# Fills and small transfers moved out of the first stage of a six-part transformer kernel

## The chip, the cores and the metric

The kernel runs on one core of one Trainium2 chip. The time is that of the device, in microseconds: 2439.63 us for the kernel before (median of 3 runs, 2437.85 to 2439.83). The core has five engines that run side by side and meet at semaphores: TensorE (PE in the profile; its weight loads are PEld), VectorE (DVE), ScalarE (ACT), GpSimd (POOL) and SyncE (SP), which here only issues transfers (DMAs).

## What is computed

The input x has 4 batches of 512 rows of 128 numbers; a context has 4 batches of 77 rows, a condition 4 rows. Four blocks follow each other, each added to x:

```python
x = x + slots(cond, ctx, layernorm(x))      # 3 steps of slot attention over the context, with a small MLP
x = x + experts(layernorm(x))               # 8 experts of 128 -> 512 -> 128, each row goes to its best 2
x = x + layers(layernorm(x), cond, ctx, masks)   # 6 layers: self attention (16 heads of 8), cross attention, MLP
x = x + ternary_mlp(x)                      # quantised 128 -> 512 -> 128

# in the slots, before the steps:
x_in  = layernorm(ctx) * g + b;  k = x_in @ wk + bk;  v = x_in @ wv + bv
slots = q_mu + exp(q_logsig) * layernorm(x)
# in the layers:
scores = where(mask, -inf, q @ k.T / sqrt(8))
```

## The kernel before, in words

x, the running state and most tables stay in SBUF for the whole kernel, as 16 tiles of 128 rows. `build` calls six stages one after the other: `load_and_prepare`, `slot_steps`, `route_tokens`, `some_experts` (the body of a loop with two turns of four experts each, so every instruction in it runs twice), `begin_layers` and `layers` (six layers, ordered by a planner, and the last MLP at its end). Each stage has a block with one program per engine. It ends when all engines are through; then GpSimd clears the stage's semaphores and a barrier follows (`stage`, L145). Inside a stage an engine runs its list in order and stops only at `wait_ge`.

**The first stage**, `load_and_prepare`:
- SyncE (L160 to L170) issues the loads in this order: x, ctx, slot rows, slot columns, slot matrices, and six constants (cond, condT, cos, sin, mask, cmask) that count up the semaphore `consts` to 96. Then (L172 to L187) it waits for VectorE's mask products, writes them to scratch in HBM, waits for that, and copies rows into the key stacks: from `shift_rows` (three partitions of -1) and from the scratch mask, 20 small transfers in all.
- GpSimd makes the identity, fills `shift_rows` (L200), small tables, the context key stack kc6 (L211), the query stacks q6 and cq (L216, four fills of 32 partitions each with ones), and the value buffers vaug and vcaug (L217 to L220). `q6`, `cq`, `vaug` and `vcaug` are first used in the layers.
- VectorE (from L262): small fills; then `dve.wait_ge(consts, 96)` and the two mask products (L267, L268); then the statistics of the context (`row_statistics`, whose lines are those of its helpers: L90, L93 moments, L100 to L102 the seed of a reciprocal root, L108 to L110 three steps of it), its normalised rows (L124), the same for the 16 tiles of x, the first slots (L282, L283), a bias (L285), and last the slots' values (L287), for which it waits for TensorE.
- TensorE turns the context and multiplies it with the key and value matrices (L243 to L255); ScalarE copies and adds biases between (L229 to L236).

**The slot steps** have no program for SyncE. VectorE starts them with L455 on the state. Every step passes the four batches from VectorE to GpSimd (roots), TensorE, ScalarE and back; L500 adds a step's output.

**The experts** have no program for GpSimd. SyncE loads the weights of four experts into `big` (L641, L642), TensorE waits for each, multiplies up (L656), ScalarE applies the gelu (L682), TensorE multiplies down (L665) and VectorE adds the share of the output to the state (L694). VectorE starts with a copy of the four experts' shares (L686).

`shift_rows` lies in the first three partitions of `big`, which the slot steps and the experts overwrite.

Of the kernel before, what the change touches and what calls it, by code (L numbers as in the profile page):

```python
# [147 lines left out]
def load_and_prepare(nc, a, m, sem):  # L148
# [2 lines left out]
    ident, ident0, lnx, lnc, ctx_ps, ctx_sb, kv_ps, kv_sb = (sem(n) for n in (  # L151
        "identity", "identity_zero", "noise_ready", "ctx_normal", "ctx_turned", "ctx_copied", "kv_ready", "kv_copied"))
    sig, dch, pch = sem("sigma"), sem("prep_dve"), sem("prep_pool")
    vu_ps, neg, neg_out, shift_out = sem("value_ready"), sem("neg_mask"), sem("neg_mask_out"), sem("shift_rows_out")
    stack0, ones = sem("stack_zero"), sem("stack_one")

    with nc.Block() as block:
        @block.sync
        def _(sp):
            sp.dma_start(m.x[:], a["x"].rearrange("b (t p) d -> p (b t) d", p=P)).then_inc(x_in, 16)  # L160
            sp.dma_start(m.ctx[0:N_CTX], a["ctx"].rearrange("b n d -> n b d")).then_inc(ctx_in, 16)
            sp.dma_start(m.rows0[:], a["slot_rows"].partition_broadcast(P)).then_inc(rows_in, 16)
            sp.dma_start(m.cols0[:], a["slot_cols"]).then_inc(mats, 16)
            sp.dma_start(m.mats0[:], a["slot_mats"]).then_inc(mats, 16)
            sp.dma_start(m.cond_rows[:], a["cond"].rearrange("b d -> (b d)").partition_broadcast(P)).then_inc(consts, 16)
            sp.dma_start(m.condT[:], a["condT"]).then_inc(consts, 16)
            sp.dma_start(m.cs[:, 0, :], a["cos"]).then_inc(consts, 16)
            sp.dma_start(m.cs[:, 1, :], a["sin"]).then_inc(consts, 16)
            sp.dma_start(m.mask_u8[:], a["mask"]).then_inc(consts, 16)
            sp.dma_start(m.cmask_u8[:], a["cmask"]).then_inc(consts, 16)  # L170

            sp.wait_ge(neg, 2)  # L172
            sp.dma_start(a["neg_mask"], m.negmask[:]).then_inc(neg_out, 16)
            sp.dma_start(a["neg_cmask"], m.negcmask[:]).then_inc(neg_out, 16)
            sp.wait_ge(neg_out, 32)

            sp.wait_ge(stack0, 1)
            sp.wait_ge(pch, 1)
            for u in range(2):
                shift, mask = u * ROW_BLOCK + ROW_SHIFT, u * ROW_BLOCK + ROW_MASK  # L180
                for i in range(2):
                    sp.dma_start(m.k6[shift:shift + 3, i], m.shift_rows[:]).then_inc(shift_out, 16)
                for b in range(B):
                    sp.dma_start(m.kc6[shift:shift + 3, b, :, 0:N_CTX], m.shift_rows[:, :, 0:N_CTX]).then_inc(shift_out, 16)
                    sp.dma_start(m.kc6[mask:mask + 1, b, :, 0:N_CTX],
                                 a["neg_cmask"][b:b + 1, :].unsqueeze(1).to_broadcast([1, PAIRS, N_CTX])).then_inc(shift_out, 16)
            sp.wait_ge(shift_out, 2 * 16 * (2 + 2 * B))  # L187
            sp.wait_ge(consts, 96)

        @block.gpsimd  # L190
        def _(pool):
            chain = Chain(pool, pch)
            pool.memset(m.ident[:], 0.0).then_inc(ident0, 1)
            pool.wait_ge(ident0, 1)
            pool.affine_select(out=m.ident[:], in_=m.ident[:], compare_op=ALU.not_equal, fill=1.0, base=0,
                               pattern=[[-1, P]], channel_multiplier=1).then_inc(ident, 1)
            pool.wait_ge(ident, 1)
            pool.tensor_copy(m.ident_bf[:], m.ident[:]).then_inc(ident, 1)

            chain.link(pool.memset(m.shift_rows[:], -1.0))  # L200

            chain.link(pool.memset(m.tri[:], 1.0))
            chain.link(pool.affine_select(out=m.tri[:], in_=m.tri[:], compare_op=ALU.is_ge, fill=0.0, base=0,
                                          pattern=[[1, P]], channel_multiplier=-1))

            chain.link(pool.memset(m.minus_half[:], -0.5))
            for e in range(EXPERTS):
                last = pool.memset(m.prefer[:, e:e + 1], float(EXPERTS - e))
            chain.link(last)

            pool.memset(m.kc6[:].rearrange("p b i n -> p (b i n)").bitcast(F32), 0.0).then_inc(stack0, 1)  # L211
            pool.wait_ge(stack0, 1)
            for q in (m.q6[:].rearrange("p i h n -> p (i h n)"), m.cq[:].rearrange("p h n -> p (h n)")):
                flat = q.bitcast(F32)
                for u in range(2):
                    chain.link(pool.memset(flat[u * ROW_BLOCK + 32:(u + 1) * ROW_BLOCK], TWO_ONES))  # L216
            chain.link(pool.memset(m.vaug[:], 0.0))  # L217
            chain.link(pool.memset(m.vcaug[:], 0.0))
            chain.link(pool.memset(m.vaug_heads[:, :, :, :, 16 + HD:17 + HD], 1.0))
            chain.link(pool.memset(m.vcaug_heads[0:N_CTX, :, :, 16 + HD:17 + HD], 1.0))  # L220

        @block.scalar
        def _(act):
# [36 lines left out]
        def _(dve):  # L260
# [2 lines left out]
            dve.memset(m.ones32[:], 1.0)  # L263
            dve.memset(m.minus_round[:], -ROUND)
            chain.link(dve.memset(m.ones[:], 1.0))
            dve.wait_ge(consts, 96)
            dve.tensor_scalar(m.negmask[:], m.mask_u8[:], MASKED, None, ALU.mult).then_inc(neg, 1)  # L267
            dve.tensor_scalar(m.negcmask[:], m.cmask_u8[:], MASKED, None, ALU.mult).then_inc(neg, 1)  # L268
            dve.wait_ge(ctx_in, 16)
            row_statistics(dve, chain, m.ctx[0:N_CTX], B, D, m.st)  # L270
            for b in range(B):
# [10 lines left out]
            chain.link(dve.tensor_tensor(m.hat[:], m.hat[:], m.sigma[:].unsqueeze(1).to_broadcast([P, T, D]), ALU.mult))  # L282
            chain.link(dve.tensor_tensor(m.state[:], m.hat[:], m.rows0[:, 0:1, :].to_broadcast([P, T, D]), ALU.add))  # L283

            dve.tensor_tensor(m.cond_rows[:], m.cond_rows[:], m.rows0[:, 5:6, :].to_broadcast([P, B, D]), ALU.add).then_inc(lnx, 1)  # L285
            dve.wait_ge(vu_ps, 1)
            dve.tensor_tensor(m.slot_v[0:N_CTX, :, 0:D], m.ps[0:N_CTX, 4, :].rearrange("n (b d) -> n b d", b=B),  # L287
# [3 lines left out]
def slot_steps(nc, a, m, sem):  # L291
# [2 lines left out]
             "root_m", "hat_m", "turned_m", "in_m", "h_ps", "h", "out_ps", "moments_p", "root_p", "hat_p", "gained", "dve", "pool")  # L294
    (moments_q, root_q, hat_q, turned_q, in_q, q_ps, q_sb, logits, mx, probs, attn, upd, moments_m, root_m, hat_m, turned_m, in_m,
     h_ps, h_sb, out_ps, moments_p, root_p, hat_p, gained, dch, pch) = [sem(f"sl_{n}") for n in names]
    scale = float(np.float32(1.0) / np.float32(D ** -0.5))

    def count(s, b):
# [3 lines left out]
        return v[:, b * TB:(b + 1) * TB]  # L303

    with nc.Block() as block:
        @block.tensor
        def _(pe):
            def turn(s, b, hat, turned):
# [323 lines left out]
def some_experts(nc, a, m, sem, turn):  # L632

    (h_ps, h_sb, o_ps, o_sb, share) = [sem(n) for n in ("ex_h_ready", "ex_h", "ex_out_ready", "ex_added", "ex_share")]
    w_in = [sem(f"ex_weights{u}") for u in range(AT_ONCE)]
    steps = [(u, b) for u in range(AT_ONCE) for b in range(B)]
    with nc.Block() as block:
        @block.sync
        def _(sp):
# [2 lines left out]
                sp.dma_start(m.proj[:, u], a["c_proj"][turn * AT_ONCE + u]).then_inc(w_in[u], 16)  # L642
            for u in range(AT_ONCE):
                sp.wait_ge(w_in[u], 32)

        @block.tensor
        def _(pe):
# [1365 lines left out]
def build(nc, a):  # L2013
    with ExitStack() as ctx:
# [40 lines left out]
        m.cmask_u8 = sb("cmask_u8", [B, N_CTX], U8)  # L2055
        m.negmask = sb("negmask", [B, S], BF16)
        m.negcmask = sb("negcmask", [B, N_CTX], BF16)
        m.shift_rows = big[0:3, 0:PAIRS * S // 2].bitcast(BF16).rearrange("r (i n) -> r i n", i=PAIRS)
        m.tri = sb("tri", [P, P], BF16)
        m.ones = sb("ones", [P, P], BF16)  # L2060
        m.invsum = {kind: sb(f"invsum_{kind}", [P, TB * 4, 2]) for kind in ("self", "cross")}
# [41 lines left out]
        m.left = m.hat[:, 2 * TB:4 * TB, :].rearrange("p (i t) d -> p i (t d)", i=2)  # L2103
        m.unit = m.xnT[:, 2:4, :]
        m.rot = sb("rot", [P, 2, 2, S])
        m.rparts = sb("rparts", [P, 2, 3, S], BF16)
        m.rot_c = sb("rot_c", [P, 2, NC_ALL])[:]
        m.rparts_c = m.cond_rows[:].rearrange("p b d -> p (b d)").bitcast(BF16)[:, 0:3 * NC_ALL].rearrange("p (k n) -> p k n", k=3)
# [119 lines left out]
```

## Time and profile before

| | before |
|---|---|
| median of 3 runs | 2439.63 us |
| the profiled execution's own time | 2435.36 us |
| its span, first to last instruction | 2433.6 us |
| TensorE busy | 2031.6 us (83%) |
| VectorE busy | 1689.8 us (69%) |
| ScalarE busy | 1537.7 us (63%) |
| GpSimd busy | 865.7 us (36%) |
| mean granted clock of TensorE | 0.919 |

The span runs from the first to the last instruction; the device's time of the same execution has a little around it (1.8 us). Busy shares are means over stages with different limits. In the rows, "L216" is line 216 of the kernel, "q<-" says what is written and from what, "x2" how many instructions a row merges; a row that merges several gives the time from the first one's start to the last one's end.

### The profile page before, as it was taken

How to read it: one execution, taken by the hardware profiler on the slowest of the kernel's cores; microseconds unless marked ns; L12 is line 12 of the kernel's file. 1: busy time of each engine (PE TensorE's matmuls, PEld its weight loads, DVE VectorE, ACT ScalarE, POOL GpSimd, SP SyncE). 2: the span in 40 equal slices, each digit the busy share in tenths (PEclk: the TensorE clock that was granted, in tenths of full speed). 3: DMA queues.
4: the chain of work that ended last, by engine and by line, in shares of the span. 5: the costliest groups of instructions: out<-in, count | busy, mean ns of one | idle time of the engine just before them, and what ended most of it. 6: DMA issues, size and time to landing. Idle time of an engine off the chain costs nothing.

```text
span 2433.6 us, 38335 instructions
## 1 busy us (share of the span) xinstructions
PE 2031.6 (83%) x14062; PEld 894.9 (37%) x14066; DVE 1689.8 (69%) x3124; ACT 1537.7 (63%) x1937; POOL 865.7 (36%) x1354
## 2 busy tenths in 40 slices
PE   2654799926889999999999999999999999988651
PEld 1332576711223333333433333333333333333321
DVE  6776211136678888888878888788878888886456
ACT  1432233303568888788778887888788878868442
POOL 4443000012234435434444344344443444433331
PEclk9776899966899999999999999999999999999665
DMA  1000101032133344332253334432353334321100
GB/s 48 1 0 1 35 1 34 0 78 56 38 65 82 80 89 84 80 88 67 68 91 88 81 82 79 92 75 61 70 108 88 74 74 93 84 54 36 32 6 9
DMA packets 148642, 144.40 MB, mean 59 GB/s; under 512 B 30887, under 2 KB 136163, under 8 KB 148451
## 3 DMA queue, kind: packets, MB, share of 16 engines
q1 hardware_dynamic: 148463, 142.05, 26.2%
q8 instruction: 108, 1.77, 0.3%
q14 instruction: 71, 0.58, 0.1%
HBM read 79.01 MB, written 60.51 MB: 57 GB/s over the span
## 4 chain that ended last, share of the span: by engine, by line
PE 56%; DVE 14%; ACT 4%; issue 3%; POOL 1%; DMA 1%; SPq 0%; POOLq 0%; DVEq 0%; ACTq 0%
PE ps L1265 14%; PE ps L1229 7%; PE ps L1218 6%; DVE smax L1763 6%; PE ps L1343 5%; PE ps L1384 4%; PE ps L1375 4%; PE ps L1277 4%; ACT big L1498 2%; PE ps L1318 2%; DVE rot L1779 2%; PE ps L1302 2%; PE ps L1240 1%; PE ps L1252 1%; PE ps L1335 1%
## 5 line engine op out<-in xcount | busy, mean ns | idle before, releaser
L1498 ACT ACTIVATE big<-ps 128x1024 f32<-128x1024 f32 x960 | 955.5, 1026 | 262.3 <-PE ps L1229 243.1
L1763 DVE TENSOR_REDUCE smax<-ps 128x2 f32<-128x1024 f32 x768 | 921.7, 1221 | 266.7 <-PE ps L1218 261.1
L1265 PE MATMUL ps<-big,vaug 128*32 128x512 f32 x3072 | 412.4, 615 | 2.9 <-ACT big L1498 2.9
L1218 PE MATMUL ps<-k,q 49*128 49x512 bf16 x1536 | 296.8, 395 | 63.7 <-DVE smax L1763 33.7
L1229 PE MATMUL ps<-q,k 52*128 52x512 bf16 x1536 | 296.5, 388 | 11.2 <-DVE smax L1763 5.4
L1694 POOL CAST mparts<-smax 128x16 bf16<-128x16 f32 x96 | 19.4, 202 | 578.1 <-DVE smax L1763 578.1
L1218 PEld LDWEIGHTS ps<-k,q 49*128 49x128 bf16 x1536 | 73.1, 94 | 313.5 <-DVE smax L1763 105.0
L694 DVE SCALAR_TENSOR_TENSOR state<-ps,share,state 128x128 f32<-128x128 f32 x128 | 36.0, 344 | 200.3 <-PE ps L665 200.3
L682 ACT ACTIVATE big<-ps 128x512 f32<-128x512 f32 x128 | 76.5, 598 | 142.9 <-PE ps L656 142.9
L1770 DVE TENSOR_REDUCE maxima<-ps 128x8 f32<-128x616 f32 x192 | 144.6, 794 | 30.7 <-PE ps L1252 29.1
L1343 PE MATMUL ps<-xnT,w 128*128 128x512 f32 x288 | 164.9, 658 | 0.9 <-ACT xnT L1535 0.9
L1229 PEld LDWEIGHTS ps<-q,k 52*128 52x128 bf16 x1536 | 75.3, 94 | 194.5 <-issue 89.9
L656 PE MATMUL ps<-xnT,big 128*128 128x512 f32 x256 | 118.0, 606 | 24.3 <-DMA big<-in_c_proj 24.3
L665 PEld LDWEIGHTS ps<-big 128*128 128x128 f32 x1024 | 119.1, 192 | 14.3 <-issue 14.3
L1685 POOL TENSOR_TENSOR hat<-rot,rparts 128x512 f32<-128x512 f32 x72 | 83.5, 1160 | 112.8 <-ACT rparts L1546 112.8
L665 PE MATMUL ps<-big 128*128 128x128 f32 x1024 | 119.2, 275 | 0.0
L1277 PE MATMUL ps<-big,vcaug 128*32 128x512 f32 x768 | 105.7, 621 | 14.2 <-ACT big L1498 7.6
L1681 POOL TENSOR_TENSOR rot<-rot 128x512 f32<-128x512 f32 x72 | 91.3, 1269 | 70.4 <-DVE rot L1779 69.0
L1667 POOL TENSOR_SCALAR var_next<-mv_next 128x4 f32<-128x4 f32 x24 | 5.6, 233 | 306.6 <-DVE mv_next L1828 306.6
L1384 PE MATMUL ps<-w,hT 128*128 128x128 f32 x768 | 109.6, 287 | 1.6 <-ACT hT L1571 1.6
L1375 PE MATMUL ps<-xnT,w 128*128 128x512 f32 x192 | 107.5, 657 | 1.9 <-ACT xnT L1535 1.9
L1691 POOL TENSOR_TENSOR rparts<-hat,rparts 128x512 bf16<-128x512 f32 x72 | 83.3, 1157 | 69.8 <-ACT rparts L1550 69.8
(290 smaller groups left out, 3026.7 us busy)
## 6 DMA issues: line engine op xcount, KB each, us to landing
q<-scratch_queries SPq DMA_DIRECT2D x48, 384.0 KB, 6.3
k<-scratch_keys SPq DMA_DIRECT2D x48, 384.0 KB
cq<-scratch_cross_queries SPq DMA_DIRECT2D x48, 384.0 KB, 5.8
scratch_queries<-rparts SPq DMA_DIRECT2D x24, 384.0 KB, 2.4
scratch_keys<-rparts SPq DMA_DIRECT2D x24, 384.0 KB, 2.6
scratch_cross_queries<-rparts SPq DMA_DIRECT2D x24, 384.0 KB, 2.5
scratch_queries<-rparts SPq DMA_DIRECT2D x24, 256.0 KB, 2.7
scratch_keys<-rparts SPq DMA_DIRECT2D x24, 256.0 KB, 3.0
```

Of the source, the lines that this page charges most:

```text
L656: nc.tensor.matmul(m.ps[:, n % 4, :], m.fc[:, u, c * P:(c + 1) * P], m.xnT[:, b, :], start=True, stop=True).then_inc(h_ps, 1)
L665: last = nc.tensor.matmul(m.ps[:, 4 + i % 2, t * P:(t + 1) * P], m.hT[:, i % 2, c, t * P:(t + 1) * P], m.proj[:, u, c, :], start=(c == 0), ...
L1218: last = nc.tensor.matmul(out[:, u], m.q6[rows, v % 2, 2 * g + pr, qt * P:(qt + 1) * P], m.k6[rows, v % 2, 2 * g + pr, :], start=True, sto ...
L1229: last = nc.tensor.matmul(out[:, u], m.k6[rows, v % 2, 2 * g + pr, kt * P:(kt + 1) * P], m.q6[rows, v % 2, 2 * g + pr, :], start=True, sto ...
L1265: last = nc.tensor.matmul(m.ps[32 * j:32 * j + 32, pv_bank, :], of_head(m.vaug, v % 2 * TB + kt, g, j), of_quad("self", q)[:, j, :], start ...
L1277: last = nc.tensor.matmul(m.ps[32 * j:32 * j + 32, aux, :], of_head(m.vcaug, v % B, g, j), of_quad("cross", n)[:, j, :], start=(g % 2 == 0 ...
L1343: got = nc.tensor.matmul(banks(kind, i)[:, half, :], w_of(m, names[half]), m.xnT[:, xn[of_turn, i], :], start=True, stop=True)
L1375: nc.tensor.matmul(banks("up", 2 * v + c // 2)[:, c % 2], w_of(m, "f1")[:, c * P:(c + 1) * P], m.xnT[:, xn["ff", v], :], start=True, stop= ...
L1384: last = nc.tensor.matmul(m.ps[:, aux, t * P:(t + 1) * P], m.hT1[:, c, t * P:(t + 1) * P], w_of(m, "f2")[:, c * P:(c + 1) * P], start=(c = ...
L1498: nc.scalar.activation(of_quad(kind, p // 2)[:, p % 2 * 2:p % 2 * 2 + 2, :], banks("exp" if kind == "self" else "cross exp", p), ACT.Exp, ...
L1763: nc.vector.tensor_reduce(m.smax[:, n % 2, qt, :, pr], banks("max", i), AX.X, ALU.max).then_inc(s_read["self"], 1)
L1770: nc.vector.tensor_reduce(m.maxima[:, qt, :, PAIRS // 2 * half:PAIRS // 2 * (half + 1)], banks("cross max", i)[:, :, 0:PAIRS // 2 * N_CTX] ...
```

## The change

The four query-stack fills and the four fills of the value buffers go from GpSimd's program in the first stage to a new GpSimd program in the experts' stage, which is executed in both turns. The 22 small transfers go from SyncE's program in the first stage to a new one in the slot steps. The mask products go from the head of VectorE's program, with their wait for `consts`, to a place behind the first slots. `shift_rows` moves from `big` to `rot`, which is first used in the layers.

```diff
@@ load_and_prepare, sync @@
-            sp.wait_ge(neg, 2)
-            sp.dma_start(a["neg_mask"], m.negmask[:]).then_inc(neg_out, 16)
-            sp.dma_start(a["neg_cmask"], m.negcmask[:]).then_inc(neg_out, 16)
-            sp.wait_ge(neg_out, 32)
-
-            sp.wait_ge(stack0, 1)
-            sp.wait_ge(pch, 1)
-            for u in range(2):
...
-            sp.wait_ge(shift_out, 2 * 16 * (2 + 2 * B))
             sp.wait_ge(consts, 96)
@@ load_and_prepare, gpsimd @@
-            pool.memset(m.kc6[:].rearrange("p b i n -> p (b i n)").bitcast(F32), 0.0).then_inc(stack0, 1)
-            pool.wait_ge(stack0, 1)
-            for q in (m.q6[:].rearrange("p i h n -> p (i h n)"), m.cq[:].rearrange("p h n -> p (h n)")):
-                flat = q.bitcast(F32)
-                for u in range(2):
-                    chain.link(pool.memset(flat[u * ROW_BLOCK + 32:(u + 1) * ROW_BLOCK], TWO_ONES))
-            chain.link(pool.memset(m.vaug[:], 0.0))
-            chain.link(pool.memset(m.vcaug[:], 0.0))
-            chain.link(pool.memset(m.vaug_heads[:, :, :, :, 16 + HD:17 + HD], 1.0))
-            chain.link(pool.memset(m.vcaug_heads[0:N_CTX, :, :, 16 + HD:17 + HD], 1.0))
+            pool.memset(m.kc6[:].rearrange("p b i n -> p (b i n)").bitcast(F32), 0.0)
@@ load_and_prepare, vector @@
             chain.link(dve.memset(m.ones[:], 1.0))
-            dve.wait_ge(consts, 96)
-            dve.tensor_scalar(m.negmask[:], m.mask_u8[:], MASKED, None, ALU.mult).then_inc(neg, 1)
-            dve.tensor_scalar(m.negcmask[:], m.cmask_u8[:], MASKED, None, ALU.mult).then_inc(neg, 1)
             dve.wait_ge(ctx_in, 16)
...
             chain.link(dve.tensor_tensor(m.state[:], m.hat[:], m.rows0[:, 0:1, :].to_broadcast([P, T, D]), ALU.add))
 
+            dve.wait_ge(consts, 96)
+            dve.tensor_scalar(m.negmask[:], m.mask_u8[:], MASKED, None, ALU.mult)
+            dve.tensor_scalar(m.negcmask[:], m.cmask_u8[:], MASKED, None, ALU.mult)
@@ slot_steps @@
     with nc.Block() as block:
+        @block.sync
+        def _(sp):
+            sp.dma_start(a["neg_mask"], m.negmask[:]).then_inc(neg_out, 16)
+            sp.dma_start(a["neg_cmask"], m.negcmask[:]).then_inc(neg_out, 16)
+            sp.wait_ge(neg_out, 32)
+            for u in range(2):
+                shift, mask = u * ROW_BLOCK + ROW_SHIFT, u * ROW_BLOCK + ROW_MASK
+                for i in range(2):
+                    sp.dma_start(m.k6[shift:shift + 3, i], m.shift_rows[:]).then_inc(shift_out, 16)
+                for b in range(B):
+                    sp.dma_start(m.kc6[shift:shift + 3, b, :, 0:N_CTX], m.shift_rows[:, :, 0:N_CTX]).then_inc(shift_out, 16)
+                    sp.dma_start(m.kc6[mask:mask + 1, b, :, 0:N_CTX],
+                                 a["neg_cmask"][b:b + 1, :].unsqueeze(1).to_broadcast([1, PAIRS, N_CTX])).then_inc(shift_out, 16)
+            sp.wait_ge(shift_out, 2 * 16 * (2 + 2 * B))
@@ some_experts @@
+        @block.gpsimd
+        def _(pool):
+            chain = Chain(pool, pch)
+            for q in (m.q6[:].rearrange("p i h n -> p (i h n)"), m.cq[:].rearrange("p h n -> p (h n)")):
+                flat = q.bitcast(F32)
+                for u in range(2):
+                    chain.link(pool.memset(flat[u * ROW_BLOCK + 32:(u + 1) * ROW_BLOCK], TWO_ONES))
+            chain.link(pool.memset(m.vaug[:], 0.0))
+            chain.link(pool.memset(m.vcaug[:], 0.0))
+            chain.link(pool.memset(m.vaug_heads[:, :, :, :, 16 + HD:17 + HD], 1.0))
+            chain.link(pool.memset(m.vcaug_heads[0:N_CTX, :, :, 16 + HD:17 + HD], 1.0))
@@ build @@
-        m.shift_rows = big[0:3, 0:PAIRS * S // 2].bitcast(BF16).rearrange("r (i n) -> r i n", i=PAIRS)
+        m.shift_rows = m.rot[0:3].rearrange("r i k n -> r (i k n)").bitcast(BF16).rearrange("r (i n) -> r i n", i=PAIRS)
```

## Rows read from the trace of the kernel before

**Rows 1.** The page: the chain of waits that ended last, by engine.
```profile
PE 56%; DVE 14%; ACT 4%; issue 3%; POOL 1%; DMA 1%; SPq 0%; POOLq 0%; DVEq 0%; ACTq 0%
```

**Rows 2.** Timeline, GpSimd, first stage: start, duration, what, how many.
```profile
6.57 1.80 POOL L211 MEMSET kc<- 128x2048 f32 x1
8.43 7.07 POOL L216 MEMSET q<- 32x4096 f32 x2
15.56 3.82 POOL L216 MEMSET cq<- 32x2048 f32 x2
19.44 3.53 POOL L217 MEMSET vaug<- 128x4112 f32 x1
...
24.90 0.31 POOL L219 MEMSET vaug<- 128x128 f32 x1
```

**Rows 3.** Timeline, VectorE, the first stage and the start of the slot steps.
```profile
12.81 2.97 DVE L267 TENSOR_SCALAR negmask<-mask_u 4x512 bf16<-4x512 uint8 x1 [11.56 <-DMA cmask_u<-in_cmask]
...
18.07 1.34 DVE L100 TENSOR_SCALAR var<-mv 77x4 f32<-77x4 f32 x1
19.44 3.55 DVE L101 TENSOR_SCALAR tmp<-var 77x4 int32<-77x4 int32 x1
23.02 1.85 DVE L102 TENSOR_SCALAR rstd<-tmp 77x4 int32<-77x4 int32 x1
24.90 0.16 DVE L108 TENSOR_TENSOR tmp<-rstd 77x4 f32<-77x4 f32 x1
...
27.78 3.19 DVE L90 BATCH_NORM_STATS2 bn<-x 128x6 f32<-128x128 f32 x16
...
32.21 0.17 DVE L100 TENSOR_SCALAR var<-mv 128x16 f32<-128x16 f32 x1
...
32.84 0.17 DVE L108 TENSOR_TENSOR tmp<-rstd 128x16 f32<-128x16 f32 x1
...
44.20 0.68 DVE L287 TENSOR_TENSOR w<-ps,w 77x512 f32<-77x512 f32 x1
45.63 0.87 DVE L455 BATCH_NORM_STATS2 bn<-state 128x6 f32<-128x128 f32 x4 [0.75 <-PEq L145]
```

**Rows 4.** Stretches (length, busy time by engine, clock, DMA, GB/s), and two loads' landing.
```profile
0.00:7.05 7.05, 0.00 (x0) 0.00 (x0) 0.37 (x4) 1.28 (x1) 5.83 (x20) 1.00 0.66 171
9.50:11.50 2.00, 0.00 (x0) 0.00 (x0) 0.00 (x0) 0.18 (x1) 2.00 (x1) 1.00 1.01 358
...
w<-in_slot_rows SPq DMA_DIRECT2D x1, 384.0 KB, 5.4
...
x<-in_x SPq DMA_DIRECT2D x1, 0.5 KB, 7.0
```

**Rows 5.** Timeline, SyncE's issues: two of the loads, first and last moved transfer.
```profile
0.86 0.92 SPq L160 DMA_DIRECT2D x<-in_x  x1
...
3.94 0.41 SPq L162 DMA_DIRECT2D w<-in_slot_rows  x1
...
17.61 0.26 SPq L173 DMA_DIRECT2D scratch_neg_mask<-negmask  x1
...
33.53 0.65 SPq L185 DMA_DIRECT2D kc<-scratch_neg_cmask  x1
```

**Rows 6.** Timeline, VectorE: the first L500 of each slot step.
```profile
82.64 0.69 DVE L500 TENSOR_TENSOR state<-state,ps 128x512 f32<-128x512 f32 x1 [6.19 <-PE ps L340]
...
138.18 0.69 DVE L500 TENSOR_TENSOR state<-state,ps 128x512 f32<-128x512 f32 x1 [6.05 <-PE ps L340]
...
195.09 0.69 DVE L500 TENSOR_TENSOR state<-state,ps 128x512 f32<-128x512 f32 x1 [6.38 <-PE ps L340]
```

**Rows 7.** Timeline, the first turn of the experts.
```profile
254.82 0.20 DVE L686 COPY share<-share 128x64 f32 x1 [0.93 <-PEq L145]
...
258.23 8.68 PE L656 MATMUL ps<-xnT,big 128*128 128x512 f32 x16 [18.48 <-DMA big<-in_c_proj]
...
270.60 1.13 DVE L694 SCALAR_TENSOR_TENSOR state<-ps,share,state 128x128 f32<-128x128 f32 x4 [15.59 <-PE ps L665]
```

More of the change, by code:

```diff
@@ L153, in load_and_prepare @@
     sig, dch, pch = sem("sigma"), sem("prep_dve"), sem("prep_pool")
-    vu_ps, neg, neg_out, shift_out = sem("value_ready"), sem("neg_mask"), sem("neg_mask_out"), sem("shift_rows_out")
-    stack0, ones = sem("stack_zero"), sem("stack_one")
+    vu_ps = sem("value_ready")
     with nc.Block() as block:
@@ L170, in _ @@
             sp.dma_start(m.cmask_u8[:], a["cmask"]).then_inc(consts, 16)
-            sp.wait_ge(neg, 2)
-            sp.dma_start(a["neg_mask"], m.negmask[:]).then_inc(neg_out, 16)
-            sp.dma_start(a["neg_cmask"], m.negcmask[:]).then_inc(neg_out, 16)
-            sp.wait_ge(neg_out, 32)
-            sp.wait_ge(stack0, 1)
-            sp.wait_ge(pch, 1)
-            for u in range(2):
[L180 to L186, printed above, removed]
-            sp.wait_ge(shift_out, 2 * 16 * (2 + 2 * B))
             sp.wait_ge(consts, 96)
@@ L296, in slot_steps @@
      h_ps, h_sb, out_ps, moments_p, root_p, hat_p, gained, dch, pch) = [sem(f"sl_{n}") for n in names]
+    neg_out, shift_out = sem("neg_mask_out"), sem("shift_rows_out")
     scale = float(np.float32(1.0) / np.float32(D ** -0.5))
@@ L636, in some_experts @@
     steps = [(u, b) for u in range(AT_ONCE) for b in range(B)]
+    pch = sem("ex_pool")
     with nc.Block() as block:
```

## The prediction

> **What bounds the kernel now.** I read the page's chain of waits first. Over the whole span TensorE holds 56% of it and VectorE 14% [rows 1], almost all in the layers, and the change touches nothing there. So its worth must be read from the stages that it does touch: the preparation, the slot steps and the experts. Next I read the preparation on the timeline, engine by engine. Until the first instruction of the slot steps (L455 at 45.63 us) the last instruction of any engine is VectorE's L287, 44.20 + 0.68 = 44.88 us [rows 3]. VectorE ends this stage; 0.75 us of barrier follow. GpSimd has done its fills at about 25.5 (the one of L219 ends at 25.21, a smaller one follows), SyncE has issued its last small transfer at 34.18 [rows 2, 5]. So the stage is worth what VectorE's chain is worth.
>
> What the reader is to see is how slowly that chain starts. VectorE waits until 12.81 us for the constants, then spends 2.97 us on the first mask product (four partitions) and 1.34, 3.55 and 1.85 us on L100 to L102 (four columns) [rows 3]. The same three lines need 0.63 us together for the sixteen tiles of x, from 32.21 to 32.84 [rows 3]. Lay the fills beside them: the second query fill ends at 8.43 + 7.07 = 15.50 and the mask product at 15.78; the cross query fills end at 19.38 and L100 at 19.41; the value fill ends at 22.97 and L101 at 22.99; the next fill begins at 24.90 and L102 ends at 24.87 [rows 2, 3]. Each waited for the end of a fill. L108 began at 24.90 together with the fill of L219 and took its usual 0.16, so not every operation is held; the tensor-scalars are.
>
> **The change part by part.** The working goes along VectorE, up to its first instruction of the slot steps.
>
> Start. The wait for the constants goes from the head of VectorE's program to near its end, so the start is set by the landing of ctx, second in SyncE's queue. Its landing isn't in the trace. Until 7.05 us the queues moved 171 GB/s x 7.05 us = 1.206 MB [rows 4], which is x (2048 x 128 x 4 B = 1.049 MB) and ctx (308 x 128 x 4 B = 0.158 MB) to the last byte if they go in order. x landed at 0.86 + 7.0 = 7.86, the slot rows, third in the queue, at 3.94 + 5.4 = 9.34 [rows 4, 5]. ctx is between these two; I take 8.2 (7.05 and some 1.1 us for the tail of a transfer). Ends: 7.86 and 9.34.
>
> Context statistics, without fills beside them (kc's fill ends at 6.57 + 1.80 = 8.37 [rows 2]). Moments: 27.78 to 32.21 for sixteen tiles is 4.43 us, so 1.1 for four, and in the slot steps the first half of it takes 0.87 (L455); with the ends of two chained groups 1.33 us. Seed, three operations: 32.21 to 32.84, 0.63 us. Three root steps and the normalise: 24.90 to 27.78, 2.88 us. Sum 4.84 us [rows 3].
>
> The part on x, unchanged: 27.78 to 44.88, 17.10 us [rows 3]. It already runs without fills. x has landed, the slot rows and matrices too.
>
> Added at its end: the two mask products, and the wait for the constants, which is met at 12.81 at the latest. A product ended 0.28 us after the fill that held it; the other is smaller, so 0.17 (L100). I take 0.5 us with the gaps. Ends: 2 x 0.17 = 0.3 us, and 2 x 0.68 (L287, 77x512) = 1.4 us [rows 3].
>
> Barrier 0.75. Together 8.2 + 4.84 + 17.10 + 0.5 + 0.75 = 31.4 us where L455 now starts at 45.63: **14.2 us earlier**. Put otherwise: 4.6 from the earlier start, 9.6 from the stalls.
>
> What is late next in this stage? TensorE and ScalarE work out slot keys and values after the context is normal; that chain waits for nothing of what is removed and moves forward with the context by over 14 us. GpSimd has nothing after 8.37; SyncE waits only for the constants at 12.81. All are more than 10 us before VectorE's end.
>
> Moved to the slot steps: SyncE's 22 transfers (two masks out to scratch, a wait for them, then 20 issues of 0.65 to 0.8 us; now from 17.61 to 34.18 [rows 5]). They take the same 17 us there, from about 31 to 48, and SyncE has no other work in that stage, which lasts until after 195 [rows 6]. Nothing is queued behind them, no engine waits for them before the layers, and they carry well under 0.2 MB. Cost nothing; with that cover gone it would be 17 us and a landing. shift_rows is now in rot instead of big, filled once in the first stage as before.
>
> Moved to the experts: eight fills on GpSimd, 8.43 to about 25.5 = 17.0 us [rows 2], and **twice**, since the stage is the body of a loop of two turns. That is 17 us more work for GpSimd, which has none there; a turn lasts 119 us (first matmul at 258.23; the second turn is alike). Who could be held? VectorE's copy L686 at 254.82, which starts with the first fill: by the nearest held rows it would end when that fill does, 3.5 us late, but its result isn't used before L694 at 270.60, a cover of 15.6 us [rows 7]. L694 itself begins at 270.60 and the fills end near 271.8; it is a scalar-tensor-tensor from PSUM, and L108 was not held; if it were, 1.2 us of one bank of two, behind which TensorE doesn't wait. TensorE and ScalarE: no row of before has a matmul beside a fill of this size. Lower end 0; upper end, see the second rival. I take 0.
>
> A placing effect remains: the same slot step is not always as long. L500 starts its steps at 82.64, 138.18 and 195.09: 55.54 and 56.91 us for the same work [rows 6], because TensorE's granted clock changes underneath. A stage that starts 14 us earlier meets other stretches. I take 0, with 1.4 us a step, 4.1 in all, either way.
>
> Sum: the profiled execution took 2435.36 us (span 2433.6); it becomes 2421.1. The median of the runs is 4.3 us above it, and the same shift gives 2439.6 - 14.2 = **2425.4 us**.
>
> **The rivals.**
>
> *The stalls have another cause (no change).* If these tensor-scalars are slow in themselves or because of transfers, then the stretch from 12.81 to 27.78 keeps its 15 us wherever its parts stand, and only the earlier start counts: 12.81 - 8.2 = 4.6 us, 2435.0 us. For it: they are the first of their kind, on integers and bytes. Against: four coincidences of an end with a fill's end within 0.3 us, and the same three lines on more columns in 0.63 us later. 4%.
>
> *The fills hold up the experts (slower).* The place: TensorE's first matmul of each turn, 3.4 us after the weights' first issue. If a fill that writes whole partitions keeps the weights' transfers or TensorE's reads out of the memory, that matmul waits for the end of the fills: 254.8 + 17.0 = 271.8 instead of 258.2, 13.6 us a turn, 27.2 in both, and 2425.4 + 27.2 = 2452.6 us. It decides the sign from 7.1 us a turn. Against it: in the first stage the transfers moved 358 GB/s from 9.50 to 11.50, with GpSimd filling for all of the 2.00 us [rows 4]. For it: no row with TensorE. 3%; a part of it, some 2 to 6 us, another 5%.
> The Trainium skill's page "SBUF — State Buffer" (section "Who interferes with whom") speaks on just this: only VectorE and GpSimd share a port pair, while transfers have ports of their own and TensorE and ScalarE never wait on anyone. By that rule this rival is worth nothing and the sum stays at 2425.4. The row on transfers agrees (358 GB/s beside a fill); for TensorE no run here shows it yet. The same section says that a VectorE operation in a two-port mode is fully blocked by a GpSimd instruction that began first, which speaks for L686 being held for up to a fill's 3.5 us in both turns, under its cover.
>
> *ctx lands later than the order of the queue says.* VectorE already waited for everything at 12.81, so the trace allows any landing up to there. Then the gain is 14.2 - 4.6 = 9.6 us and the time 2430.0. Against: the byte count, and x and the slot rows on both sides of it. 5%.
>
> *The clock eats or adds to it.* All three steps on their bad side: 2429.5; on their good side: 2421.3. This is in my range.
>
> **How the numbers follow.** The forecast, 2425.4 with its own 2421 to 2430, has 83%; the late ctx 5%, a part of the experts' cost 5%, the full cost 3%, no stall removed 4%. Range: down by the clock's 4.1 to 2421; up by the clock, the later end of ctx (1.1) and the dearer products (0.9), 2431, which takes the late ctx in. A measurement of this kernel tells changes over about 0.2% (4.9 us) from none, so faster means under 2434.7: the forecast, late ctx and most of the partial cost, 93%. Within: the stall rival and the rest of the partial, 4%. Slower: 3%.
>
> **What would show it.** In the changed profile L90 on ctx starts near 8.2, L100 to L102 take 0.2 us each, the mask products stand near 30 us at under 0.7 each, and L455 first starts near 31.4. GpSimd shows eight fills in each turn and the turns' first matmuls still come 3.4 us after the weights' issue; L686 shows 0.2 or up to 3.5 us. A turn stays near 119 us. I am wrong if L100 to L102 stay over 1 us, if ctx is waited for until 10 us or later, or if a turn grows by more than 1 us.

## The result, and the profile after

The change made the kernel faster, by some 0.6%. In runs side by side its median was 2422.31 us (9 runs, 2414.46 to 2432.63) against 2437.76 us (9 runs of the kernel before, 2431.71 to 2440.06): ratio 0.9939, 95% interval 0.9923 to 0.9955. Timed a second time it was 2425.70 against 2439.76 us, 0.9935 (0.9916 to 0.9954). The forecast was 2425.4, a ratio of 0.9942 to the 2439.63 it started from.

The profiled execution took 2431.73 us with a span of 2430.0, so the two profiled executions differ by 3.6 us and not by 15. The medians explain it: the one of the kernel before, 2435.36, lies 2.4 us below the median of 2437.76, the one of the changed kernel 9.4 us above that of 2422.31. Where in the kernel those microseconds lie is answered below.

VectorE in the first stage of the changed kernel (timeline: start, duration, line, what, how many, idle time before it and what ended that); these rows answer to [rows 3]:

```profile
9.39 0.87 DVE L90 BATCH_NORM_STATS2 bn<-ctx 77x6 f32<-77x128 f32 x4 [8.15 <-DMA ctx<-in_ctx]
...
10.70 0.17 DVE L100 TENSOR_SCALAR var<-mv 77x4 f32<-77x4 f32 x1
10.90 0.17 DVE L101 TENSOR_SCALAR tmp<-var 77x4 int32<-77x4 int32 x1
11.10 0.17 DVE L102 TENSOR_SCALAR rstd<-tmp 77x4 int32<-77x4 int32 x1
...
14.18 3.19 DVE L90 BATCH_NORM_STATS2 bn<-x 128x6 f32<-128x128 f32 x16
...
29.99 0.42 DVE L257 TENSOR_SCALAR negmask<-mask_u 4x512 bf16<-4x512 uint8 x1
30.33 0.18 DVE L258 TENSOR_SCALAR negcmask<-cmask_u 4x77 bf16<-4x77 uint8 x1
...
31.04 0.67 DVE L261 TENSOR_TENSOR w<-ps,w 77x512 f32<-77x512 f32 x1
32.45 0.87 DVE L445 BATCH_NORM_STATS2 bn<-state 128x6 f32<-128x128 f32 x4 [0.74 <-PEq L145]
```

L100 to L102 take 0.17 us each where they took 1.34, 3.55 and 1.85; the idle time at the head ends with the landing of ctx and not with that of the constants; the slot steps start at 32.45 instead of 45.63, 13.2 us earlier.

The moved transfers, first and last issue, on SyncE's timeline of the changed kernel, against [rows 5]:

```profile
32.41 0.25 SPq L283 DMA_DIRECT2D scratch_neg_mask<-negmask  x1
...
48.36 0.66 SPq L292 DMA_DIRECT2D kc<-scratch_neg_cmask  x1
```

Their issue ends 150 us before the slot steps do. The moved fills in the first turn of the experts, with the copy of the shares and TensorE's first matmuls (timelines of GpSimd, VectorE and TensorE), against [rows 2, 7]:

```profile
241.12 7.07 POOL L643 MEMSET q<- 32x4096 f32 x2 [38.99 <-POOLq L145]
...
257.42 0.33 POOL L646 MEMSET vaug<- 128x128 f32 x1
```

```profile
241.37 3.31 DVE L689 COPY share<-share 128x64 f32 x1 [0.93 <-PEq L145]
```

```profile
244.88 8.62 PE L659 MATMUL ps<-xnT,big 128*128 128x512 f32 x16 [18.58 <-DMA big<-in_c_proj]
```

The copy went from 0.20 to 3.31 us: it ends at 244.68, two hundredths after the first of the two query fills (241.12 + 7.07/2 = 244.66). Nobody waited for it: VectorE's next instruction, the first L697 at 257.19, had sat idle for another 12.51 us until TensorE was through. TensorE started 3.51 us after the copy's start, before it was 3.41.

**Where one execution loses its gain.** The start of each stage by VectorE's first instruction, from the timelines of all ten profiles (us; the experiments are told below). The last column is the length of the layers, with the last MLP:

| kernel | slot steps | routing | turn 1 | turn 2 | to the layers | end of span | layers: end of span minus their start |
|---|---|---|---|---|---|---|---|
| before | 45.63 | 216.60 | 254.82 | 374.62 | 493.73 | 2433.6 | 1939.9 |
| changed | 32.45 | 203.14 | 241.37 | 361.22 | 482.05 | 2430.0 | 1948.0 |
| changed, again | 31.88 | 202.38 | 240.61 | 360.42 | 479.50 | 2425.9 | 1946.4 |
| fills moved alone | 36.17 | 206.35 | 247.67 | 368.84 | 488.65 | 2432.6 | 1944.0 |
| order alone | 43.15 | 214.37 | 252.60 | 372.46 | 493.29 | 2434.5 | 1941.2 |
| transfers back | 48.34 | 220.24 | 258.45 | 380.20 | 500.13 | 2440.5 | 1940.4 |
| fills doubled | 32.07 | 202.49 | 240.71 | 360.54 | 481.40 | 2426.1 | 1944.7 |
| fills in the routing | 31.54 | 202.40 | 246.75 | 366.85 | 486.17 | 2426.0 | 1939.8 |
| ctx first | 27.34 | 197.42 | 238.73 | 359.87 | 479.65 | 2420.1 | 1940.5 |
| ctx first, long fills first | 26.98 | 198.45 | 236.66 | 356.54 | 477.39 | 2415.3 | 1937.9 |

The gain is whole at the start of turn 2 (13.4 us). The second turn then took 120.8 us instead of 119.1, and the layers 8.1 us more than in the one profile of the kernel before. The first 16.4 us of the second turn follow, for the kernel before and the changed kernel. A row gives the stretch, its length, the busy times of TensorE, its weight loads, VectorE, ScalarE and GpSimd with the number of instructions of each, TensorE's granted clock as a share of full speed, and the share and GB/s of the transfers:

```profile
374.62:391.00 16.38, 13.07 (x51) 7.88 (x52) 1.02 (x5) 5.72 (x9) 0.00 (x0) 0.90 0.38 128
```

```profile
361.22:377.60 16.38, 12.98 (x43) 7.22 (x44) 3.13 (x1) 5.70 (x9) 15.98 (x8) 0.79 0.38 128
```

The same 16.38 us were granted 0.90 of full speed before and 0.79 after, and fewer matmuls were through (51 and 43). The fills are not the reason. The same stretch of the kernel "order alone", whose experts have no fills, and then of the changed kernel profiled again, whose experts have them:

```profile
372.46:388.84 16.38, 12.99 (x43) 7.20 (x44) 0.19 (x1) 5.70 (x9) 0.00 (x0) 0.79 0.40 128
```

```profile
360.42:376.80 16.38, 13.08 (x51) 7.87 (x52) 3.98 (x5) 5.71 (x10) 15.98 (x8) 0.90 0.38 128
```

Without fills the clock was 0.79 here, with fills 0.90. In the layers I followed one of the losses, 3.5 of the 8.1 us. Two marks one layer apart (the same ScalarE row of the chain, at 1480.72 and 1762.01) lie 281.3 us apart, and 277.8 before. Three neighbouring stretches of the changed kernel between them:

```profile
1491.00:1501.00 10.00, 9.73 (x76) 3.76 (x74) 8.68 (x20) 7.91 (x11) 4.68 (x8) 1.00 0.74 161
1501.00:1511.00 10.00, 8.10 (x42) 2.13 (x36) 5.00 (x8) 4.92 (x6) 7.50 (x12) 0.83 0.85 62
1511.00:1521.00 10.00, 9.87 (x52) 4.11 (x56) 7.24 (x7) 8.53 (x11) 3.29 (x7) 1.00 0.19 66
```

The middle one again in the kernel before, at the same distance from the mark:

```profile
1510.31:1520.31 10.00, 8.95 (x63) 2.71 (x56) 7.34 (x10) 6.91 (x9) 7.68 (x12) 1.00 0.67 57
```

The clock is at 0.83 against 1.00, with 42 matmuls through instead of 63. The second profile of the same kernel has 278.1 us between the marks. So the end of one span can't judge this change; the start of the slot steps can, to some tenths.

### The profile page after: what moved, and what is told of

It reads as the page before. It is cut to its first block, busy times and chain, and to the rows that moved or that the text cites. A ratio compares the mean times of both kernels' runs of the same rounds, so it can differ in the third digit from the quotient of the medians.

```text
span 2430.0 us, 38348 instructions
## 1 busy us (share of the span) xinstructions
PE 2038.2 (84%) x14066; PEld 897.6 (37%) x14066; DVE 1686.1 (69%) x3124; ACT 1538.0 (63%) x1937; POOL 882.0 (36%) x1362
## 4 chain that ended last, share of the span: by engine, by line
PE 56%; DVE 14%; issue 4%; ACT 4%; POOL 1%; DMA 1%; SPq 0%; POOLq 0%; DVEq 0%; ACTq 0%
PE ps L1268 14%; PE ps L1232 7%; PE ps L1221 6%; DVE smax L1766 6%; PE ps L1346 6%; PE ps L1387 4%; PE ps L1378 4%; PE ps L1280 4%; ACT big L1501 2%; DVE rot L1782 2%; PE ps L1321 2%; PE ps L1305 2%; PE ps L1243 1%; PE ps L1255 1%; PE ps L1338 1%
## 5 line engine op out<-in xcount | busy, mean ns | idle before, releaser
L697 DVE SCALAR_TENSOR_TENSOR state<-ps,share,state 128x128 f32<-128x128 f32 x128 | 36.0, 344 | 196.0 <-PE ps L668 196.0
L668 PEld LDWEIGHTS ps<-big 128*128 128x128 f32 x1024 | 119.1, 192 | 14.4 <-issue 14.4
L1268 PEld LDWEIGHTS ps<-big,vaug 128*32 128x32 f32 x3072 | 63.7, 109 | 117.8 <-issue 95.4
```

Source lines behind the costliest of these rows:

```text
L668: last = nc.tensor.matmul(m.ps[:, 4 + i % 2, t * P:(t + 1) * P], m.hT[:, i % 2, c, t * P:(t + 1) * P], m.proj[:, u, c, :], start=(c == 0), ...
L1268: last = nc.tensor.matmul(m.ps[32 * j:32 * j + 32, pv_bank, :], of_head(m.vaug, v % 2 * TB + kt, g, j), of_quad("self", q)[:, j, :], start ...
```

## The experiments

**The changed kernel again.** No edit.

> The changed kernel once more, unchanged. Theory: the first stage is fixed by one landing and one chain, so the first instruction of the slot steps starts at 32.5 us again, within 0.3. What differs from run to run lies in the layers. In the first look at it the gain over the kernel before was 13.2 us at the start of the slot steps, 13.4 at the start of the second turn of experts, 11.7 at the start of the layers and 3.6 at the end. If that loss is chance, this look ends with another loss (between 0 and 10 us) at other places, and the ratio to the kernel before is 0.994 to 0.995. Rival: the moved work costs something in the layers or in the second turn (its 1.7 us), then the same loss stands at the same places again.

It began the slot steps at 31.88, 0.6 us earlier than in the first profile and 0.3 outside what was expected, because ctx landed at 8.81. The gain stood at 13.8 us there, 14.2 at the start of the layers and 7.7 at the end. Turn 2 took 119.1, the stretch with 281.3 us took 278.1: the first profile's losses were not at the same places. But the layers took 1946.4 us, again longer than the 1939.9 of the kernel before. Over all ten profiles they took 1937.9 to 1948.0, and the kernels with the fills in the experts' stage have both ends of that range. The three without them (before, order alone, fills in the routing) took 1939.8 to 1941.2, though, and four of the seven with them 1944.0 or more, so ten profiles alone don't exclude that the fills cost the layers a few us. The medians speak against it: the gain in them, 15.4 and 14.1 us, is not smaller than the 13.2 and 13.8 us at the start of the slot steps; their intervals, from 11 us up, leave room for 2 to 3 us all the same. What follows: the stage's gain is stable, and what the layers add or take in one execution is a scatter of up to 10 us.

**The fills moved, the order of VectorE as before.** The transfers stay moved too.

```diff
             chain.link(dve.memset(m.ones[:], 1.0))
+            dve.wait_ge(consts, 96)
+            dve.tensor_scalar(m.negmask[:], m.mask_u8[:], MASKED, None, ALU.mult)
+            dve.tensor_scalar(m.negcmask[:], m.cmask_u8[:], MASKED, None, ALU.mult)
             dve.wait_ge(ctx_in, 16)
...
-            dve.wait_ge(consts, 96)
-            dve.tensor_scalar(m.negmask[:], m.mask_u8[:], MASKED, None, ALU.mult)
-            dve.tensor_scalar(m.negcmask[:], m.cmask_u8[:], MASKED, None, ALU.mult)
```

> The wait for the constants and the two mask products go back to the head of VectorE's program; the fills stay with the experts and the transfers with the slot steps. Theory (the fills held the tensor-scalars): the products start at 12.8 and take 0.42 and 0.18 us, L100 to L102 take 0.2 each, and the slot steps start at 12.8 + 0.5 + 4.8 + 17.1 + 0.75 = 35.9 to 36.0 us, 3.5 later than in the changed kernel and 9.7 earlier than before; median about 2426. Rival (the early operations are slow for another reason, the start of the chain was the gain): the products take 3.0 and 1.9 us again and the slot steps start at 40 us or later.

VectorE on the timeline of this kernel:

```profile
13.10 0.42 DVE L241 TENSOR_SCALAR negmask<-mask_u 4x512 bf16<-4x512 uint8 x1 [11.85 <-DMA cmask_u<-in_cmask]
...
14.85 0.17 DVE L100 TENSOR_SCALAR var<-mv 77x4 f32<-77x4 f32 x1
...
36.17 0.87 DVE L445 BATCH_NORM_STATS2 bn<-state 128x6 f32<-128x128 f32 x4 [0.74 <-PEq L145]
```

The products and L100 are short although VectorE's order is that of the kernel before: with it the slot steps start 9.5 us earlier. That this is the fills' and not the moved transfers', the next kernel shows. Median 2425.63, ratio 0.9943 (0.9922 to 0.9964); this can't be told from the 2425.70 of the changed kernel timed beside it, so the 3.7 us between the two stand on the starts of the slot steps (36.17 and 32.45), not on the medians. Its routing took 41.3 us instead of 38.2, 3.1 lost again, and here the line is plain. The instructions of the routing's small matmuls, this kernel and then the one before (durations min/median/max in ns, first and last start):

```profile
L549 PE MATMUL ps<-wg,xnT x32: 221/361/361, 220.8 to 227.2; 128*128 128x8 f32 x32
```

```profile
L559 PE MATMUL ps<-wg,xnT x32: 175/256/361, 230.9 to 234.4; 128*128 128x8 f32 x32
```

The 32 of them took 6.83 us together instead of 3.90, most at 361 ns instead of 256 and under; from 223.0 to 227.7 the granted clock was 0.50, the lower level of 1.2 GHz, against 0.91 before in the like stretch (230.8 to 234.8).

**The order alone.** The fills stand in the first stage again and are gone from the experts.

```diff
-            pool.memset(m.kc6[:].rearrange("p b i n -> p (b i n)").bitcast(F32), 0.0)
+            chain.link(pool.memset(m.kc6[:].rearrange("p b i n -> p (b i n)").bitcast(F32), 0.0))
+            for q in (m.q6[:].rearrange("p i h n -> p (i h n)"), m.cq[:].rearrange("p h n -> p (h n)")):
...
+            chain.link(pool.memset(m.vcaug_heads[0:N_CTX, :, :, 16 + HD:17 + HD], 1.0))
```

> The eight fills go back to the first stage, in the old order behind the fill of the context keys; the mask products stay late and the transfers stay in the slot steps. Theory (a fill that is running holds a tensor-scalar until it ends): the context's statistics start at 9.4, but L100, L101 and L102 end at 12.0, 15.5 and 17.4 to 19.4 with the ends of fills, the four normalising tensor-scalars are held by the value fills, and the context is done only at about 25; the slot steps start at 43 to 44 us, so the new order alone is worth about 2 us and the median is about 2436. Rival (the earlier start is worth its 3.4 us whatever the fills do): the slot steps start at 42.2 or earlier, in any case with L100 to L102 at under 0.3 us each.

VectorE and GpSimd on the timeline of this kernel:

```profile
8.45 0.87 DVE L90 BATCH_NORM_STATS2 bn<-ctx 77x6 f32<-77x128 f32 x4 [7.20 <-DMA ctx<-in_ctx]
...
9.76 2.20 DVE L100 TENSOR_SCALAR var<-mv 77x4 f32<-77x4 f32 x1
12.00 3.53 DVE L101 TENSOR_SCALAR tmp<-var 77x4 int32<-77x4 int32 x1
15.56 1.82 DVE L102 TENSOR_SCALAR rstd<-tmp 77x4 int32<-77x4 int32 x1
17.42 0.16 DVE L108 TENSOR_TENSOR tmp<-rstd 77x4 f32<-77x4 f32 x1
...
19.15 5.70 DVE L124 TENSOR_SCALAR w<-ctx,mv,rstd 77x128 f32<-77x128 f32 x4
```

```profile
8.43 7.07 POOL L198 MEMSET q<- 32x4096 f32 x2
15.56 3.65 POOL L198 MEMSET cq<- 32x2048 f32 x2
19.27 3.53 POOL L199 MEMSET vaug<- 128x4112 f32 x1
22.86 1.84 POOL L200 MEMSET vcaug<- 128x2064 f32 x1
```

This is the clearest picture of the mechanism, and the transfers have no part in it: none of the 22 is issued before 43.11 us. L100 ends at 11.96 with the first query fill, L101 at 15.53 with the second (15.50), L102 at 17.38 with the first cross query fill, and the four normalising operations, 1.11 us elsewhere, take 5.70 and end at 24.85 behind the value fills. Nine operations of the root from 17.42 on run beside fills in their usual 0.16 us. The moments, L90 at 8.45, ran beside the first query fill in their usual 0.87. The context's part of the chain starts 4.4 us earlier than the products did before and is done 2.9 us earlier; the slot steps start at 43.15, 2.5 us earlier. Median 2435.41, ratio 0.9984 (0.9971 to 0.9996). Its second turn of experts, in which GpSimd does nothing, took 120.8 us: the 1.7 us that the changed kernel's first profile lost there are not the fills'.

**The transfers back in the first stage**, behind the late products, and gone from the slot steps.

```diff
+            sp.wait_ge(neg, 2)
+            sp.dma_start(a["neg_mask"], m.negmask[:]).then_inc(neg_out, 16)
...
+            sp.wait_ge(shift_out, 2 * 16 * (2 + 2 * B))
             sp.wait_ge(consts, 96)
```

> The 22 small transfers go back to the first stage, behind the mask products, which stay at their late place. Theory: SyncE can start them only at 30.5 us; the two writes with their wait take 1.5, the 20 issues 14.9, the last landing 1 to 2, so the first stage ends near 49 and the slot steps start at about 50 us, 17.5 later than in the changed kernel and later than before (45.6); median about 2440. So the move of the transfers is worth nothing by itself, but the late place of the products can't do without it. Rival: the wait for them is short or they overlap, and the slot steps start before 40 us.

SyncE's last issue, and VectorE's first instruction of the slot steps:

```profile
45.60 0.65 SPq L185 DMA_DIRECT2D kc<-scratch_neg_cmask  x1
```

```profile
48.34 0.87 DVE L445 BATCH_NORM_STATS2 bn<-state 128x6 f32<-128x128 f32 x4 [17.57 <-PEq L145]
```

VectorE sat idle for 17.57 us until the others were through. The slot steps start 1.7 us earlier than the 50 that I expected and 2.7 us later than before; median 2441.72, ratio 1.0004 (0.9989 to 1.0020): the whole gain is gone. With the products at their late place, worth 3.7 us, the transfers' move is needed. With the products at the head it may not be: that kernel was not run, but before, the last issue ended 16.6 us after the products (17.58 to 34.18), which without the fills end at 13.6 us (13.44 + 0.18), so that all would be issued by 30.2 and VectorE's end at 35.4 us would still come last. This is an estimate from the rows of the kernel before and of the one with the fills moved alone.

**The fills doubled** in the experts, 34 us in each turn.

```diff
-            for q in (m.q6[:].rearrange("p i h n -> p (i h n)"), m.cq[:].rearrange("p h n -> p (h n)")):
...
+            for _ in range(2):
+                for q in (m.q6[:].rearrange("p i h n -> p (i h n)"), m.cq[:].rearrange("p h n -> p (h n)")):
...
```

> The changed kernel with the eight fills of the experts' stage done twice in each turn: 34 us of fills from the turn's start, 68 in all. Theory (only VectorE's tensor-scalars and copies are held, and the experts have none but the copy of the shares): the copy is held for up to 3.5 us as in the changed kernel, TensorE's first matmul still comes 3.5 us after the turn's start, a turn lasts 119.1 to 121.8 us as the turns seen so far, with and without fills, and the median is that of the changed kernel within 0.2%. Rival (the fills are in the way of TensorE, ScalarE or the weights): whatever they cost now is doubled, a turn is longer than 122 us in both turns.

TensorE's first matmuls of the first turn:

```profile
244.22 8.61 PE L660 MATMUL ps<-xnT,big 128*128 128x512 f32 x16 [18.58 <-DMA big<-in_c_proj]
```

That is 3.51 us after the copy's start, as with half the fills. The turns took 119.83 and 120.86 us; without any fills they take 119.11 to 120.83 (before and order alone). VectorE's scalar-tensor-tensors (L698) took their 1.13 us for four beside the fills, as without them. Median 2422.84, ratio 0.9935 (0.9922 to 0.9949), the same as the changed kernel's. 34 us of fills more cost nothing that can be measured.

**The fills in the routing**, once.

```diff
@@ some_experts @@
-        @block.gpsimd
...
@@ route_tokens @@
+        @block.gpsimd
+        def _(pool):
+            chain = Chain(pool, pch)
+            for q in (m.q6[:].rearrange("p i h n -> p (i h n)"), m.cq[:].rearrange("p h n -> p (h n)")):
...
```

> The eight fills go from the experts to the routing stage, once instead of twice. VectorE runs that stage alone for most of its 38.2 us, with tensor-scalars on x (L100 to L102, 16 of L124) and copies. Theory (fills hold tensor-scalars, not the statistics): the moments are done 6.7 us after the stage's start, when 10 us of fills are left; L100 to L102 end with the ends of fills, some of the normalising ones too, and the stage takes 42 to 46 us, so this place costs 4 to 8 us that the experts' place doesn't. Rival (any stage is as good as another, since GpSimd is idle): the stage stays at 38.2 us.

VectorE in that stage:

```profile
209.16 0.30 DVE L100 TENSOR_SCALAR var<-mv 128x16 f32<-128x16 f32 x1
209.50 1.82 DVE L101 TENSOR_SCALAR tmp<-var 128x16 int32<-128x16 int32 x1
211.35 1.82 DVE L102 TENSOR_SCALAR rstd<-tmp 128x16 int32<-128x16 int32 x1
...
215.09 6.75 DVE L124 TENSOR_SCALAR hat<-x,mv,rstd 128x128 f32<-128x128 f32 x16
```

3.4 us are lost at L100 to L102 and 2.6 at L124 (4.19 without fills). The stage took 44.35 us instead of 38.2. Median 2429.12, ratio 0.9960 (0.9946 to 0.9973). The fills doubled, timed beside it, had a median of 2422.84: 6.3 us less, about the 6.1 us that the routing grew. That GpSimd idles in a stage does not make the place free.

**ctx ahead of x**, a step beyond the change.

```diff
-            sp.dma_start(m.x[:], a["x"].rearrange("b (t p) d -> p (b t) d", p=P)).then_inc(x_in, 16)
             sp.dma_start(m.ctx[0:N_CTX], a["ctx"].rearrange("b n d -> n b d")).then_inc(ctx_in, 16)
+            sp.dma_start(m.x[:], a["x"].rearrange("b (t p) d -> p (b t) d", p=P)).then_inc(x_in, 16)
```

> The changed kernel with the load of ctx issued ahead of that of x. Theory (the landing of ctx is the start of everything): ctx, 0.16 MB and alone, lands at 4.5 to 5.5 us instead of 8.4 to 9.4; the context's moments are done at about 6.3; of L100 to L102 one or two are held by the fill of the context keys until 8.4, so the context is done at about 11.5 instead of 13.2 to 14.2. x lands by 9.5, before it is wanted. The slot steps start at 29.5 to 30 us, 2 to 3 us earlier, median about 2421. Rival (x lands later by as much, or the order of the issues doesn't decide the landing): they start at 31.9 or later.

```profile
3.45 0.87 DVE L90 BATCH_NORM_STATS2 bn<-ctx 77x6 f32<-77x128 f32 x4 [2.20 <-DMA ctx<-in_ctx]
...
4.76 0.60 DVE L100 TENSOR_SCALAR var<-mv 77x4 f32<-77x4 f32 x1
```

The context's statistics start at 3.45 us, a microsecond earlier than expected, so early that they are past L102 before the fill of the context keys begins at 6.57. L100 took 0.60 us instead of 0.17 and ended with the fill of the shift rows (5.36 and 5.33); the four normalising operations, beside the fill of the context keys, took 1.44 instead of 1.11. The slot steps start at 27.34, 5.1 us earlier than in the changed kernel's first profile. Median 2417.88, ratio to the kernel before 0.9916 (0.9902 to 0.9930). My expected 2 to 3 us were too few.

**ctx first, and GpSimd's long fills first.**

```diff
+            pool.memset(m.kc6[:].rearrange("p b i n -> p (b i n)").bitcast(F32), 0.0)
+            chain.link(pool.memset(m.rot[0:3].rearrange("r i k n -> r (i k n)"), TWO_MINUS_ONES))
             pool.memset(m.ident[:], 0.0).then_inc(ident0, 1)
...
-            chain.link(pool.memset(m.shift_rows[:], -1.0))
...
-            pool.memset(m.kc6[:].rearrange("p b i n -> p (b i n)").bitcast(F32), 0.0)
```

> As the kernel with ctx first, and GpSimd begins with its two long fills: the context keys (1.8 us), then the shift rows, filled as pairs in half the elements (1.8 instead of 3.5 us); the identity and the small tables follow. Theory: no long fill is left when the tensor-scalars on the context come, so that they take 0.2 us each and the context is done 4.8 us after the landing of ctx, at 9.5 to 10.3; x has landed by 9.5. The slot steps start at 27.8 to 28.6 us, 4 us earlier than in the changed kernel, median about 2419. Rival (x becomes what is waited for): the statistics of x start only at 10.5 or later, and half of the gain is gone.

```profile
8.71 3.19 DVE L91 BATCH_NORM_STATS2 bn<-x 128x6 f32<-128x128 f32 x16 [0.38 <-DMA x<-in_x]
```

No tensor-scalar is held any more: L101 to L103 (L100 to L102 in the other kernels) take 0.17 us each and the normalising 1.11. But now the statistics of x wait for x, 0.38 us, and whatever else would speed up the context would only lengthen this wait. The slot steps start at 26.98, nearly a microsecond earlier than expected. Median 2418.44, ratio 0.9915 (0.9902 to 0.9929), not to be told from the step before. Both beat the changed kernel by some 2 thousandths, worked out from two ratios to the same kernel before (0.9916 and 0.9915 against 0.9939 and 0.9935). The intervals of these ratios overlap; what carries the step is the start of the slot steps, and that of the ten runs of the two kernels only the slowest (2421.83) was not faster than all five of the fills doubled (2421.74 to 2427.78), timed beside them.

## Why the prediction was right

**What was right and what was luck.** The mechanism, the removal of the stalls and the earlier start, came as forecast, and the slot steps start 13.2 and 13.8 us earlier where 14.2 was put. That the medians came within 0.001 of the forecast ratio is partly luck: they differ by 15.4 and 14.1 us, and their intervals allow from 11 to 19 and from 11 to 20. For the profiled execution itself the prediction put 2421.1 us; it took 2431.73, 10.6 more: some 8.1 of them in the layers and 1.7 in the second turn, for which it put nothing, and 1.0 in the first stage.

**The start of the chain** was the term most in error in this stage. I took ctx at 8.2 us; VectorE could start on it at 9.39 in the first profile and at 8.44 to 9.01 in the others that load it second. x and the slot rows on both sides of it gave 9.34 as the upper end, which one profile passed by 0.05: the loads themselves were later there (the slot rows let ScalarE go at 10.10 instead of 9.37). The count of bytes was no good guide to the landing: by 7.05 us the first profile had moved more of them (176 GB/s x 7.05 us = 1.24 MB) than the kernel before, and yet ctx came 1.2 us later than I took; no run shows the 1.1 us that I put for the tail of a transfer. So 1.2 us of the 14.2 were missing by this, and small differences in the other terms gave 0.1 back.

**The stalls.** 4.84 us for the context without fills; measured 14.18 - 9.39 = 4.79. Order alone and fills alone separate the two terms. The prediction's 9.6 for the stalls stands against 9.5 with the old order (and 10.7 with the new one, 43.15 to 32.45, although ctx came 0.9 us later in the latter). Its 4.6 for the earlier start exists only with the fills away: it is 3.7 us then (36.17 to 32.45), and 2.5 us with the fills in place, because the chain only reaches the next fill sooner. The two parts don't add up singly; whichever comes second is worth more.

**x and the products.** 27.78 to 43.59 before and 14.18 to 29.99 after: 15.81 us both times. The products took 0.45 us with overlap, 0.5 was put. The barrier 0.74.

**The moved transfers** cost nothing in the slot steps, which took 170.7 us against 171.0. Putting them back showed the price without cover, 17.57 us of idle time with the barrier's 0.74 in it, so 16.8, where the prediction said 17 and a landing.

**The moved fills** cost nothing although they run twice. The doubled fills refute the rival that had them in TensorE's way: neither turn is more than 0.03 us longer than the longest one without fills. One of the prediction's own signs of being wrong did appear: the second turn of the first profile grew from 119.11 to 120.83 us, more than 1 us. It stands for the clock and not for the fills, since it is also 120.83 in order alone, which has no fills there, and 119.08 in the changed kernel profiled again. The copy was held as the rows of the first stage suggested, 3.31 and 3.13 us in the two turns, and its cover of 15.6 us made it free. By the Trainium skill ("SBUF — State Buffer", "Who interferes with whom") TensorE and the transfers should not notice a fill; 244.22 as TensorE's start with doubled fills, 3.51 us after the copy's there and in the changed kernel alike, agrees.

**The clock.** Put at 0 with 4.1 us either way, for the slot steps. There the ten profiles differ by 1.8 us (170.1 to 171.9), and a single step takes about 55.5 or 57.0 us: 55.54 and 56.91 before, 55.49 and 56.87 in the changed kernel, 57.00 and 55.67 with the fills moved alone. So the 1.4 us a step was of the right size. But other stages, for which nothing was put, move more: the routing can lose 3.1 us, a turn 2.0 (the first one, 119.80 to 121.75) and a layer 3.5. The differences of the medians of many runs, 15.4 and 14.1 us, stay near the forecast of 14.2. Whether a little of those is the layers' own can't be said from runs that scatter by 8 to 18 us.

## What to carry to other kernels

When a small VectorE operation ends, time after time, just when a GpSimd fill beside it ends, and takes a fraction of that elsewhere, move the fill and not only the operation; and move it beside work whose VectorE operations are none of the held kinds (here, but for one copy under cover, scalar-tensor-tensors from PSUM), not simply to a stage where GpSimd is idle. Before a wait is moved later, look who feeds on its result in the same stage: here 17 us of small transfers hung on it. A change of a few thousandths is judged in a profile by where the changed stage ends, not by the end of the span, and beside that by the medians of many runs.

## What the runs showed beside this

- The place of the ctx load in the queue was worth more than its size suggests: 0.16 MB behind 1.05 MB landed at 8.4 to 9.4 us, ahead of it at 3.45.
- The routing stage has two lengths, 38.2 and 41.3 us, with the same instructions: TensorE's 32 small matmuls run either mostly at 256 ns and under or mostly at 361 ns, at the lower granted clock. Which of them an execution gets is not explained by anything I changed; two profiles of ten had the long one (fills moved alone, and ctx first). The ten profiles include one with the fills in this stage, whose routing took 44.35 us for another reason, told above.
